# A state-space scan whose carried product is split over the two halves of TensorE's rows

## What is computed

```python
def step(S, inp):
    dA_t, dt_t, B_t, C_t, x_t = inp
    S = S * dA_t[:, :, None, None] + jnp.einsum('bh,bn,bhp->bhpn', dt_t, B_t, x_t)
    y_t = jnp.einsum('bhpn,bn->bhp', S, C_t)
    return (S, y_t)
...
y = ys.transpose(1, 0, 2, 3) + D_param[None, None, :, None] * xh
y = y * jax.nn.silu(z.reshape(Bb, Ll, NHEADS, HEADDIM))
return y.reshape(Bb, Ll, D_MODEL) @ W_out.T
...
x = x + _layernorm(attn(_layernorm(x)))
x = x + _layernorm(down(silu(gate(_layernorm(x))) * up(_layernorm(x))))
```

## Time and profile before

| | us |
|---|---|
| median of 3 runs | 1351.74 |
| profiled execution | 1352.4 |
| its span, first to last instruction | 1350.7 |
| TensorE busy | 1298.0 |
| DVE busy | 945.4 |
| ACT busy | 553.8 |
| POOL busy | 491.4 |

### The profile page before, as it was taken

How to read it: one execution, slowest core, us unless ns; L and a number is a source line. 1 busy time by engine, 2 the same in 40 slices (tenths; PEclk the granted TensorE clock), 3 DMA queues, 4 the chain that set the end, 5 groups by cost and what they waited for, 6 DMA issues and landing times. The chain is left out here.

```text
span 1350.7 us, 18988 instructions
## 1 busy us (share of the span) xinstructions
PE 1298.0 (96%) x6796; PEld 639.4 (47%) x6796; DVE 945.4 (70%) x1921; ACT 553.8 (41%) x1042; POOL 491.4 (36%) x701
## 2 busy tenths in 40 slices
PE   4889999999999999999999999999999999999997
PEld 2445555554445445544444444544544445444443
DVE  7878889995687668865787568756886556544332
ACT  5666867785434243433433233424342222122120
POOL 1313233233433543454443543353435444401102
PEclk9998999999999999999999999999999999999999
DMA  5055337324302422133212330233014102302201
GB/s 175 20 99 137 87 88 149 100 67 106 87 24 52 113 63 56 32 90 97 65 32 54 88 86 25 63 109 86 25 33 116 47 25 63 108 17 37 73 0 55
DMA packets 132813, 96.17 MB, mean 71 GB/s; under 512 B 102000, under 2 KB 102000, under 8 KB 132720
## 3 DMA queue, kind: packets, MB, share of 16 engines
q1 hardware_dynamic: 124752, 78.74, 22.8%
q10 hardware_dynamic: 7968, 16.23, 4.7%
HBM read 54.05 MB, written 16.78 MB: 52 GB/s over the span
## 5 line engine op out<-in xcount | busy, mean ns | idle before, releaser
L1524 PE MATMUL bank<-fxt,ffn_hi 128*128 128x512 f16 (+1 forms) x1408 | 419.2, 379 | 7.0 <-DVE gact L1914 5.6
L1524 PE MATMUL bank<-fxt,ffn_lo 128*128 128x512 f16 (+1 forms) x704 | 267.0, 379 | 0.0
L1524 PEld LDWEIGHTS bank<-fxt,ffn_hi 128*128 128x128 f16 (+1 forms) x1408 | 139.4, 100 | 173.8 <-DVE gact L1914 9.9
L1538 PE MATMUL bank<-ffn_hi,h_hi 128*128 128x512 f16 (+1 forms) x352 | 133.6, 380 | 0.0
L1538 PE MATMUL bank<-ffn_hi,h_lo 128*128 128x512 f16 (+1 forms) x352 | 133.5, 379 | 0.0
L1538 PE MATMUL bank<-ffn_lo,h_hi 128*128 128x512 f16 (+1 forms) x352 | 133.4, 379 | 0.0
L1409 PE MATMUL bank<-mask,diag 128*128 128x416 f16 x640 | 122.4, 347 | 6.5 <-ACT ffn_lo L958 4.1
L656 POOL TENSOR_TENSOR state<-state,ex 64x512 f32<-64x512 f32 x32 | 36.6, 1144 | 226.8 <-PE bank L1478 225.6
L1914 DVE SCALAR_TENSOR_TENSOR gact<-gact,bank 128x512 f32<-128x512 f32 (+1 forms) x88 | 60.3, 685 | 82.9 <-ACT gact L1010 81.9
L1010 ACT ACTIVATE gact<-bank,c_gate_half 128x512 f32<-128x512 f32 (+1 forms) x88 | 59.9, 681 | 142.2 <-PE bank L1524 140.4
L1783 DVE SCALAR_TENSOR_TENSOR xs<-cin,conv_w_sb,xs 128x512 f32<-128x512 f32 x114 | 103.3, 907 | 17.3 <-ACT xs L899 14.2
(11 more groups left out here) (197 smaller groups left out, 2251.2 us busy)
## 6 DMA issues: line engine op xcount, KB each, us to landing
codes_sb<-codes ACTq DMA_DIRECT2D x76, 208.0 KB, 3.5
ures<-u SPq DMA_DIRECT2D x32, 256.0 KB, 2.9
x_scratch<-x SPq DMA_DIRECT2D x32, 256.0 KB, 2.4
ut<-x_scratch SPq DMA_DIRECT2D x16, 512.0 KB, 4.5
xres<-x_scratch SPq DMA_DIRECT2D x32, 256.0 KB, 2.9
out<-dn SPq DMA_DIRECT2D x32, 256.0 KB, 2.0
ut<-u SPq DMA_DIRECT2D x15, 512.0 KB, 4.4
ffn_hi<-w_in_t SPq DMA_DIRECT2D x4, 580.0 KB, 8.7
```

The lines of the kernel that those rows point to most:

```text
L1524: last = nc.tensor.matmul(bank, wt[:, c0:c0 + w], fxt[:, :, half, k, :], start=(k == 0 and n == 0), stop=(k == KC - 1 and n == 2))
L1538: last = nc.tensor.matmul(banks[FFN_BANKS[turn % 3]][:], h[0:w, m, tok], wt[0:w, d0:d0 + D], start=(m == 0 and n == 0), stop=(m == MB - 1 ...
```

## The change

The state becomes [128, 256]: heads 0 to 3 in partitions 0 to 63, heads 4 to 7 in partitions 64 to 127, for even and odd tiles alike. The carried product is now two products of 64 rows and 256 columns: one reads the lower partitions and writes bank 4, the other reads the upper partitions and writes bank 5. C stands in only one half of the partitions, so ACT copies a chunk of it to the other half (cpair, 64x128) at the end of small_sums. Each head's inner product goes to the second half of the bank that holds its head's carried product, and accumulates there without a start of its own. The decay over the whole chunk is needed for other heads in the lower and the upper partitions: the last of the three sums is four matmuls of 64 weight columns and 4 moving columns in the place of two of 128 and 8. y_sum waits for the inner products first and then works bank by bank. POOL multiplies the state as 128x256. The state update is one DVE addition, and at the end of a sequence (odd tile, last chunk) a memset in its place; clear_state in the stages falls away.

```diff
--- before.py
+++ after.py
@@ -223,11 +223,14 @@
         decay = sb("decay", [P, HEADS, P])
         gram = sb("gram", [P, P + NST])
         bt = gram[:, P:P + NST]
-        ex = sb("ex", [P, 3, HEADS])
+        ex = sb("ex", [P, 2 * HEADS + HEADS // 2])
+        ex_in, ex_out, ex_all = ex[:, 0:HEADS], ex[:, HEADS:2 * HEADS], ex[:, 2 * HEADS:]
         xtok = sb("xtok", [P, D])
         xdt = sb("xdt", [P, D])
         xd = sb("xd", [P, D])
-        state = sb("state", [P, D])
+
+        state = sb("state", [P, D // 2])
+        cpair = sb("cpair", [P, P])
         y = sb("y", [P, D])
         ymax = sb("ymax", [P, 1])
         yexp = sb("yexp", [P, SUB])
@@ -272,8 +275,14 @@
 
         dve_passed = sem("dve_waits_passed")
         banks = [ctx.enter_context(nc.psum_tensor(f"bank{i}", [P, 512], F32)) for i in range(8)]
-        tok_bank, carried_bank, inner_bank = banks[2], banks[4], banks[5]
-        seg_banks = (banks[4], banks[5])
+        tok_bank = banks[2]
+
+        def halves_of(t):
+
+            half = t % HALVES
+            return slice(half * NST, (half + 1) * NST), slice((1 - half) * NST, (2 - half) * NST)
+
+        seg_banks = y_banks = (banks[4], banks[5])
 
         raw = ffn_hi[:].bitcast(F32)
         w_in_f = raw[:, 0:KC * D_IN].rearrange("p (k n) -> p k n", k=KC)
...
@@ -641,12 +651,11 @@
                     xw_ready.inc(nc.gpsimd.tensor_tensor(
                         xtok[:].rearrange("p (h d) -> p h d", h=HEADS),
                         xdt[:].rearrange("p (h d) -> p h d", h=HEADS),
-                        ex[:, 1, :].unsqueeze(2).broadcast_to((P, HEADS, HD)), ALU.mult))
+                        ex_out.unsqueeze(2).broadcast_to((P, HEADS, HD)), ALU.mult))
 
                 def decay_state(t, c):
-                    h0 = t % HALVES * NST
-                    if h0 == 0 and c == 0:
-                        pool.wait_ge(state_cleared.sem, state_cleared.now(t // HALVES, 1))
+                    if t == 0 and c == 0:
+                        pool.wait_ge(state_cleared, 1)
                     else:
                         pool.wait_ge(state_ready.sem, state_ready.prev(t, SUB + c))
                     pool.wait_ge(yi_done.sem, yi_done.now(t, c + 1))
@@ -654,9 +663,8 @@
                     if c == 0 and t > LAG:
                         pool.wait_ge(res_ready.sem, res_ready.now(t - 1 - LAG, SUB))
                     stated.inc(nc.gpsimd.tensor_tensor(
-                        state[h0:h0 + NST, :].rearrange("p (h d) -> p h d", h=HEADS),
-                        state[h0:h0 + NST, :].rearrange("p (h d) -> p h d", h=HEADS),
-                        ex[h0:h0 + NST, 2, :].unsqueeze(2).broadcast_to((NST, HEADS, HD)), ALU.mult))
+                        state[:].rearrange("p (h d) -> p h d", d=HD), state[:].rearrange("p (h d) -> p h d", d=HD),
+                        ex_all.unsqueeze(2).broadcast_to((P, HEADS // 2, HD)), ALU.mult))
                     pool.wait_ge(stated.sem, stated.now(t, c + 1))
 
                 def out_rstd(t, c):
@@ -983,8 +991,12 @@
                     p = place(t - 1, "sN") if c == 0 else place(t, f"s{c}")
                     act.wait_ge(p.filled, p.n + 1)
                     sums_ready.inc(nc.scalar.activation(
-                        ex[:], p.bank[:, 192:216].rearrange("p (k h) -> p k h", k=3), ACT.Exp, scale=1.0 / SEG))
+                        ex[:], p.bank[:, 192:212], ACT.Exp, scale=1.0 / SEG))
                     nc.scalar.activation(gram[:], p.bank[:, 0:P + NST], ACT.Copy).then_inc(p.freed, 1)
+                    here, other = halves_of(t)
+                    if t > 0 or c > 0:
+                        act.wait_ge(yi_done.sem, yi_done.now(t, c))
+                    cpair_ready.inc(nc.scalar.activation(cpair[other, :], cs[here, c * P:(c + 1) * P], ACT.Copy))
 
                 def decays(t, c):
                     act.wait_ge(seg_done.sem, seg_done.now(t, c + 1))
@@ -1438,10 +1450,15 @@
                     nc.tensor.matmul(p.bank[:, 0:P], bs[h, tok], cs[h, tok], start=True, stop=True)
                     nc.tensor.transpose(p.bank[:, 128:192], bs[h, tok], ident[h, h])
                     pe.wait_ge(dt_steps.sem, dt_steps.now(t, 20))
-                    for n, sums in enumerate((causal_h, below_h, ones_h)):
+                    for n, sums in enumerate((causal_h, below_h)):
                         for piece in range(2):
-                            last = nc.tensor.matmul(p.bank[:, 192 + n * HEADS:192 + (n + 1) * HEADS], sums[:],
-                                                    da[:, half, c, piece, :], start=(piece == 0), stop=(piece == 1))
+                            nc.tensor.matmul(p.bank[:, 192 + n * HEADS:192 + (n + 1) * HEADS], sums[:],
+                                             da[:, half, c, piece, :], start=(piece == 0), stop=(piece == 1))
+                    for g in range(2):
+                        for piece in range(2):
+                            last = nc.tensor.matmul(p.bank[g * NST:(g + 1) * NST, 208:212], ones_h[:, 0:NST],
+                                                    da[:, half, c, piece, 4 * g:4 * g + 4],
+                                                    start=(piece == 0), stop=(piece == 1))
                     last.then_inc(p.filled, 1)
 
                 def segment_sums(t, c):
@@ -1464,29 +1481,36 @@
 
                     pe.wait_ge(decay_ready.sem, decay_ready.now(0, 2))
                     for _ in range(n):
-                        nc.tensor.matmul(carried_bank[:], ident_h[:], win_hi[:, 0, 0:D], start=True, stop=True)
+                        nc.tensor.matmul(y_banks[0][:], ident_h[:], win_hi[:, 0, 0:D], start=True, stop=True)
 
                 def scan(t, c):
                     dec = t < LAG
                     tok = slice(c * P, (c + 1) * P)
+                    here, other = halves_of(t)
                     half = t % HALVES
-                    h = slice(half * NST, (half + 1) * NST)
-                    if half == 0 and c == 0:
-                        pe.wait_ge(state_cleared.sem, state_cleared.now(t // HALVES, 1))
+                    if t == 0 and c == 0:
+                        pe.wait_ge(state_cleared, 1)
                     pe.wait_ge(state_ready.sem, state_ready.prev(t, SUB + c))
                     pe.wait_ge(decay_ready.sem, decay_ready.now(t, 2 * c + 2))
-                    yi_done.inc(nc.tensor.matmul(carried_bank[:], cs[h, tok], state[h, :], start=True, stop=True))
+                    pe.wait_ge(cpair_ready.sem, cpair_ready.now(t, c + 1))
+                    for g in range(2):
+                        rows = slice(g * NST, (g + 1) * NST)
+                        last = nc.tensor.matmul(y_banks[g][:, 0:D // 2], cs[rows, tok] if g == half else cpair[rows, :],
+                                                state[rows, :], start=True, stop=False)
+                    yi_done.inc(last)
                     if dec:
                         if t == 0 and c == 0:
                             pe.wait_ge(s_ddiag, 2)
                         for k in range(KC):
-                            nc.tensor.matmul(inner_bank[:, k * P:(k + 1) * P], xs[:, half, k, tok], d_diag[:, k, :],
-                                             start=(k == 0), stop=False)
+                            at = D // 2 + k % 2 * P
+                            nc.tensor.matmul(y_banks[k // 2][:, at:at + P], xs[:, half, k, tok], d_diag[:, k, :],
+                                             start=False, stop=False)
                     pe.wait_ge(xdt_ready.sem, xdt_ready.now(t, c + 1))
                     pe.wait_ge(mt_ready.sem, mt_ready.now(t, c + 1))
                     for n in range(HEADS):
-                        last = nc.tensor.matmul(inner_bank[:, n * HD:(n + 1) * HD], decay[:, n, :],
-                                                xdt[:, n * HD:(n + 1) * HD], start=not dec, stop=not dec or n == HEADS - 1)
+                        at = D // 2 + n % 4 * HD
+                        last = nc.tensor.matmul(y_banks[n // 4][:, at:at + HD], decay[:, n, :],
+                                                xdt[:, n * HD:(n + 1) * HD], start=False, stop=n % 4 == 3)
                     y_done.inc(last)
                     p = place(t - 1, "sN") if c == 0 else place(t, f"s{c}")
                     pe.wait_ge(p.freed, p.n + 1)
@@ -1853,23 +1877,23 @@
                     dve.wait_ge(y_steps.sem, y_steps.now(t, YSTEPS * c + k))
 
                 def y_sum(t, c):
-                    half = t % HALVES
-                    h = slice(half * NST, (half + 1) * NST)
-                    dve.wait_ge(yi_done.sem, yi_done.now(t, c + 1))
-                    y_step(t, c, 1, nc.vector.tensor_tensor(
-                        y[:].rearrange("p (h d) -> p h d", h=HEADS),
-                        carried_bank[:].rearrange("p (h d) -> p h d", h=HEADS),
-                        ex[:, 0, :].unsqueeze(2).broadcast_to((P, HEADS, HD)), ALU.mult))
                     dve.wait_ge(y_done.sem, y_done.now(t, c + 1))
```

(23 more changed lines are left out.)

12 lines of the change are left out of this document (6 added, 6 removed).

## The result

The changed kernel takes 1344.41 us (median of five runs, 1342.84 to 1350.62), the kernel before 1351.74 (five runs, 1350.38 to 1354.99): a ratio of 0.9939, 95% interval 0.9913 to 0.9965. It is faster by 0.6%, and the prediction of 1346.0 us (1341 to 1356) holds. The profiled execution is the slowest of the five, 1350.62 us, so its span must not be set against the median. The two traces are compared by stretches instead.

The account below looks back on a forecast made before the run. TensorE, busy 96% of the span, was taken to bound the kernel. Six stages at -0.97 us (-5.8) and +0.1 before 332 us make -5.7: 1352.4 to 1346.7 profiled, 1346.0 us as median, range 1341 to 1356.

Parts of the forecast that it names:

- The carried product: TensorE in scan: two products of 64 rows in different array rows run side by side, -0.43 us a scan.
- The argument from L1495's columns to the new rows: L1495's two products in different columns overlap, 0.43 us instead of 0.85; the new pair in different rows should too.
- No overlap: Rival: the row halves in scan run one after the other, nothing saved, layout changes remain; 1358 us, chance 0.12.
- half an overlap: Rival: only two of the four passes in scan meet, 0.21 us saved a scan; 1351.5 us, chance 0.16.
- weight loads one after the other: Rival: serial weight loads on TensorE cost 0.10 us more a scan; 1348.7 us, chance 0.15.
- The sums: TensorE in prepare: four 64-column matmuls change the layout and back, +0.25 us a prepare, bounds +0.05 and +0.36.
- cheap layout change: Rival: the layout change of the sums in prepare costs only 0.05 us; 1341.3 us, chance 0.10.
- The stall: TensorE's one wait per stage, for gate_silu: its chain starts from up(g, 0), so it absorbs prepare(t, 1)'s +0.25 us.
- y_sum, absorbed for the reason given: DVE after scan: y_sum ends 0.56 us later, but h_lo behind it waits for POOL's segments anyhow, so no cost.
- The copies on ACT: ACT's cpair copy takes about 0.28 us, hidden in the stages; without cover, 0.28 us each.
- The stretch before 332 us: Masks and decode share the engines, so TensorE's savings are largely waited away: +0.1 us, bounds -1.2 and +2.5.
- the wait for y_sum(0, 1) grows: TensorE's longest early wait, 4.9 us, before L1453 at 102 us, grows by 0.4 us or more.

Follow-up runs that it names:

- the sums in the full layout: Changed kernel with the four whole-chunk sum matmuls taking 128 weight columns of ones_h padded with zeros, accumulating in the same four columns; 1349.40 us in one execution.
- the addition held: Kernel before the change, with y_sum made to wait for all of scan ahead of its multiplication; 1349.96 us in one execution.
- the products apart: Changed kernel with the second carried product issued in the middle of the inner products from tile 2 on; 1365.23 us in one execution.

## Why the prediction was right, and where not

**The carried product, right.** Predicted -0.43 a scan by full overlap, measured 1.052 to 0.632, -0.42. The argument from L1495's columns to the new rows held. No overlap (1358), half an overlap (1351.5) and weight loads one after the other (1348.7) fall with the pairs of starts at 513.68 and 513.69. The Trainium skill's strict program order (TensorE: Matmul & The Clock Gate, Part 3, "What overlaps and what doesn't") would, with a product's two passes together in the program, have left the first product's second pass ahead of the second product's first. The starts show the passes in pairs. Whether they already stand so in the program or the chip pairs them, no trace here shows; so the rule alone doesn't tell how two float32 products in different rows are started. That tiles in different rows run side by side, as the same part says, does hold: 0.63 us for the pair and 0.63 for one.

**The sums, right in kind, a third too dear.** Predicted +0.25, measured +0.18, and 0.195 with what the segment sums lose. From the start of the last below_h sum to the segment sums it was 0.075 us and is 0.26: 0.10 up to the first new sum, 0.06 over the four of them, 0.10 to the segment sums. So the two changes cost the 0.10 that I took. The loads between them cost 0.06 rather than 0.10, and the 0.025 that any two of these tiny matmuls stood apart before is contained in the first change, which I had not taken off. The rival of a cheap layout change (0.05 us more a prepare) falls.

**The stall, wrong: the step that failed** is "That chain starts from up(g, 0), read at 485.21, not from the scan ... its +0.25 us only eats into the stall". What I read is one of two inputs. The other, from segment_sums through ACT and POOL to the instruction of DVE that POOL holds up, is the later one in most stages, in the kernel before as well, and moves with prepare. The stall, 1.29 us in stage 2 and 1.08 in the four others before, is 1.19, 1.22, 1.08, 1.22 and 1.11 after, +0.045 on average; the sums in the full layout show all four prepares paid. The sum with what was measured: 4 x -0.42 + 4 x 0.195 + 0.045 = -0.855 us a stage, where -0.85 was measured; and for the last stage, with three prepares and no stall, 4 x -0.42 + 3 x 0.195 = -1.10, as measured. Mine was -0.97 a stage: the prepare too dear (4 x 0.25 instead of 4 x 0.195, +0.22), one prepare wrongly absorbed (-0.25), the stall's growth left out (-0.045) and 0.01 too much saved on each scan (-0.04). The errors nearly cancelled, and the total of -5.8 against -5.4 is right partly by luck.

**y_sum, absorbed for the reason given, the size off.** Predicted 0.56 us later against the inner products, measured 0.23. Two instructions of 256 columns without a wait between start 0.34 us apart, not 0.42 (two of 419 ns span 0.76 and 0.75 us in the rows). After scan(3, 1) h_lo starts only 0.1 us later against POOL's segments and shrinks from 1.78 to 1.68:

```profile
516.35 0.76 DVE L1882 TENSOR_TENSOR y<-bank,ex 128x256 f32<-128x256 f32 x2 [1.81 <-PE bank L1512]
517.14 0.75 DVE L1889 TENSOR_TENSOR y<-y,bank 128x256 f32<-128x256 f32 x2
...
519.07 1.68 DVE L1954 TENSOR_TENSOR h_lo<-hf,h_hi 128x512 f16<-128x512 f32 x1
```

The later start of y_sum on the kernel before confirmed the absorption with more delay than the change has. No wait for gate_silu came after scan(t, 1).

**The copies on ACT, nearly right.** Predicted 0.28 and hidden, measured 308 ns; hidden in the even stages, while the odd ones lost 0.14 us by it. decay_state fell to 0.66 us, not quite half of 1.14.

**The stretch before 332 us, open.** Predicted +0.1 (-1.2 to +2.5). scan(2, 0) starts at 331.60 and 335.04 in the first two traces; over the three traces of before and its two variants the mean is 331.3, over the eight of the change and its variants 332.4, and the single ones reach from 328.6 to 336.6. An effect of a microsecond can't be read from that. The granted clock goes with part of it: ahead of 328 us it averages 0.98 in the earliest trace (the addition held, 328.6) and 0.95 in the latest (the sums in the full layout, 336.6), but it is 0.96 in both traces of the change, which lie 3.6 us apart. The step that said the wait for y_sum(0, 1) grows is neither borne out nor refuted (4.9 us before, 3.7 and 6.6 after); what else moved there I did not settle.

## What to carry to other kernels

Two small float32 products were had for the price of one here, since they read different rows of the array and stand directly behind each other; with half of the inner products between them the gain was gone. A matmul in another layout than its neighbours cost a tenth of a microsecond each way, so try tiny ones padded with zeros to the neighbours' layout. Before a stall is counted as cover for an addition, follow each input of its last instruction back to where it leaves the bounding engine: if the later one leaves behind the addition, the stall covers nothing. Here it was the order of one queue that made the stall at all.

## What the runs showed of the hardware

- The passes of two float32 products in different rows interleave in pairs, starts 513.68 and 513.69, then 514.00 and 514.01: a second product is free (0.63 us with it and without it).
- Four tiny matmuls of 64 weight columns between ones of 128 cost 0.18 us more than the two they replaced, padded to 128 columns 0.05.
- A DVE instruction of 1.23 us with both inputs in SBUF (decayed) that starts while one of POOL runs ends 1.08 us after that one has ended (1.11 at most, in the stages t = 2 to 6 of both kernels): it shows up to 1.95 us. In one case (the products apart, t = 2) where the two started 0.04 us from each other, POOL's waited instead (2.13 us for 1.04).
- A stretch with many engines in play, the first 330 us, scatters by 8 us (328.6 to 336.6) between kernels that differ little, and by 3.6 between two traces of the same kernel, whereas the stages behind it repeat within 0.03 us in those two. In other kernels a late ut or a drop of the clock moved single stages, by 3 us at most.
